# Second attention hands its tiles to the scan inside SBUF; first quarter's norm coefficients alone; softplus by tanh

## The chip, the cores and the metric

One core of one Trainium2 chip runs the whole program. The metric is the device time of one execution in microseconds (us); lower is better. The engines are PE (TensorE, matrix multiply), DVE (VectorE), ACT (ScalarE), POOL (GpSimd) and SP (SyncE, which here only issues DMA transfers and waits). Each runs its own instruction stream; semaphores order them.

## The reference

Two layers work on x of 128 batches x 32 steps x 128 features. What the change touches is the end of the second layer's attention and the preparation of its selective scan:

```python
x = x + _L1_xattn_ref(_layernorm(x), ctx, ctx, Wq, bq, Wk, bk, 32, 0)   # attention over 257 context rows
x = x + _L1_attn_ref(_layernorm(x), W_in, conv_w, conv_b, W_x, W_dt, b_dt, A_log, ...)
...
xc, z = (xz[..., :256], xz[..., 256:])          # xz = x @ W_in.T
u = silu(conv over 4 steps of xc + conv_b)
x_dbl = u @ W_x.T                               # 33 columns: 1 for dt, 16 for B, 16 for C
dt = jnp.clip(jax.nn.softplus(dt_raw @ W_dt.T + b_dt), 0.0001, 10.0)
A = -jnp.exp(jnp.minimum(A_log, 5.0))
y = scan over the 32 steps with 16 states per channel, from u, dt, A, B, C
```

Softplus is log(1 + exp(v)). It equals max(v, 0) + log(1 + exp(-|v|)), and also max(v, 0) - log(0.5 + 0.5 tanh(|v| / 2)).

## The kernel before

The stages run one after another: first attention, mixer, experts (layer 0), second attention (`stage_cross1`), then `stage_scan1`, which calls `scan_inputs`, `scan_states` and `stage_tail`. Between stages all engines meet at a barrier and the semaphores are cleared.

**Two layouts.** Up to the second attention a tile of x is 4 batches x 32 steps on the 128 partitions, and there are 32 tiles: `g.x[128, 32, 128]`, where partition b\*32+s of tile t is step s of batch 4t+b. The scan wants the 128 batches on the partitions and the 32 steps as its 32 tiles. Before, the second attention writes each finished tile to a DRAM tensor (`x_mid`, line 1465, one DMA of 64 KB per tile), and `scan_inputs` reads it back into `g.x` in four DMAs of 512 KB, a quarter of the steps each (line 1659).

**The second attention** is a software pipeline over 32 tiles (`step(t, p)` on each engine). SP's step, in this order: the last context row of tile t (line 1446, 4 rows of 512 B into one partition); in odd steps a context tile for t+2 (line 1395) and its transpose for t+4 (line 1389), half a megabyte each; then the output of tile t-3. Even tiles find their context in SBUF already. The waits are for `o_psum` (attention of tile t-2 done, so that a buffer is free), `scores_psum` and `x_sb` (tile t-3 written). SP runs the step in a hardware loop.

**The preparation of the scan** (`scan_inputs`) starts with the layer norm: DVE takes `bn_stats` of the 32 tiles as they land, then eight small instructions and one Sqrt on ACT give the coefficients of all tiles (`norm_coefficients`). Eight weight loads are issued by ACT (`w_in`, 8 loads); when all are in, DVE folds the convolution taps into the input weights (`w_c`, line 1794) and splits the bias row (lines 833 to 841, the last one `si_cb`). PE waits for all that (`prep`), then runs one tile per step: transpose of the normed tile, convolution and gate as matmuls into `c_ps`, transpose of u, `W_x` product. ACT applies Silu (line 1705), copies the transposed tile (line 1708) and writes |v| of dt into `soft` (Abs, line 1712); DVE copies uT and xd, and computes v = w_dt \* xd + b_dt (line 1785); POOL copies u and z out and prepares gates for the first 12 tiles.

**After the last tile** comes the softplus in four quarters of 8 tiles, in two halves, and the clip:

```python
for half in range(2):
    for q in quarters: activation(soft, soft, ACT.Exp, scale=-1.0)      # L1733
    for q in quarters: activation(soft, soft, ACT.Ln, bias=1.0)         # L1737
...
vec.scalar_tensor_tensor(dt, dt, 0.0, soft, ALU.max, ALU.add)           # L1802
vec.tensor_scalar(dt, dt, 1e-4, 10.0, ALU.max, ALU.min)                 # L1804
```

DVE then negates `a` (line 1806), and the stage ends. `scan_states` follows: ACT first makes 24 products `come` (line 1907), then exponentials `decay` (line 1897) for each step.

Of the kernel before, what the change touches and what calls it, by code (L numbers as in the profile page):

```python
# [1397 lines left out]
def stage_cross1(nc, g):  # L1398
# [7 lines left out]
    with ExitStack() as ctx:  # L1406
# [30 lines left out]
        def _(sp):  # L1437
# [182 lines left out]
def scan_inputs(nc, g, uz, dt, xd, a):  # L1620


    with ExitStack() as ctx:
# [25 lines left out]
        waited, abs_sb, exp_sb, ln_sb, soft_sb, clip_sb = (sem(n) for n in ("waited", "abs_sb", "exp_sb", "ln_sb", "soft_sb", "clip_sb"))  # L1649
        block = ctx.enter_context(nc.Block())  # L1650
# [4 lines left out]
        @block.sync  # L1655
        def _(sp):
            for q in range(XQ):
                t = slice(q * QT, (q + 1) * QT)
                sp.dma_start(g.x[:, t, :], g.x_mid[:, t, :]).then_inc(x_in[q], 16)
            load_tail_rows(g, sp)  # L1660
            sp.wait_ge(g.tail.rows_in, 16 * 3)
            sp.wait_ge(g.tail.loaded, 16 * 4)

        @block.tensor
        def _(pe):
# [29 lines left out]

            pe.wait_ge(prep, TAPS + 2 + 9)
            pipeline(pe, step, 2, 1, TAPS)

        @block.scalar
        def _(act):  # L1700
            def step(t, p):
# [24 lines left out]
            act.wait_ge(abs_sb, T)  # L1726
            act.wait_ge(a_step, 1)
            nc.scalar.activation(a[:, :], a[:, :], ACT.Exp).then_inc(a_step, 1)
            for half in range(2):
                quarters = range(half * LN_Q // 2, (half + 1) * LN_Q // 2)  # L1730
                for q in quarters:
                    s = slice(q * LT, (q + 1) * LT)
                    nc.scalar.activation(soft[:, s, :], soft[:, s, :], ACT.Exp, scale=-1.0).then_inc(exp_sb, 1)  # L1733
                for q in quarters:
                    s = slice(q * LT, (q + 1) * LT)
                    act.wait_ge(exp_sb, q + 1)
                    nc.scalar.activation(soft[:, s, :], soft[:, s, :], ACT.Ln, bias=1.0).then_inc(ln_sb, 1)  # L1737

# [31 lines left out]
        def _(dve):  # L1770
            vec = nc.vector

            def step(t, p):
# [7 lines left out]
                if inside(t - 1):  # L1781
# [3 lines left out]
                    vec.scalar_tensor_tensor(dt[:, t - 1, :], w_dt[:, :], xd[:, t - 1, 0:1], b_dt[:, :],  # L1785
                                             ALU.mult, ALU.add).then_inc(dt_sb, 1)
# [4 lines left out]
            vec.memset(cb[:, :], 0.0).then_inc(prep, 1)  # L1791
            dve.wait_ge(w_in, 16 * W_LOADS)
# [3 lines left out]
            dve.wait_ge(prep, 2)  # L1796
            split_row(vec, dve, prep, TAPS + 2, cb3[:, :], rowmask, (c_hi[:, :], c_rest[:, :], c_f[:, :]), cb[0:3, :])
            pipeline(dve, step, 3, 1, TAPS)
            for q in range(LN_Q):
                s = slice(q * LT, (q + 1) * LT)  # L1800
                dve.wait_ge(ln_sb, q + 1)
                vec.scalar_tensor_tensor(dt[:, s, :], dt[:, s, :], 0.0, soft[:, s, :], ALU.max, ALU.add).then_inc(soft_sb, 1)  # L1802
                dve.wait_ge(soft_sb, q + 1)
# [3 lines left out]
            dve.wait_ge(clip_sb, LN_Q)  # L1807

# [782 lines left out]
def build(nc, dram, out):  # L2591
    with ExitStack() as ctx:
# [11 lines left out]
        with ExitStack() as early:  # L2604
            sb = tensor_makers(nc, early, "early")[0]
            g.w_uv, g.w_eo = sb("w_uv", [P, 2, E1]), sb("w_eo", [P, CB, D])
            g.uvb, g.ob = sb("uvb", [P, 2 * E1], BF16), sb("ob", [P, D])
            g.filt, g.dft, g.idft = sb("filt", [FR, E1]), sb("dft", [P, 3, S]), sb("idft", [FR, S])
            g.w_g, g.w_u, g.w_d = sb("w_g", [P, HC, P]), sb("w_u", [P, HC, P]), sb("w_d", [P, HC, D])
            g.w_r, g.spread0 = sb("w_r", [P, NE]), sb("spread0", [P, RC, P], BF16)  # L2610
            g.w_q, g.w_k, g.cross_cols = sb("w_q", [P, D]), sb("w_k", [P, D]), sb("cross_cols", [P, 2])
# [3 lines left out]
            with ExitStack() as kept:  # L2615
# [92 lines left out]
```

## Time and profile before

| | us |
|---|---|
| median of 3 runs (lowest 1869.15, highest 1873.27) | 1869.2 |
| the profiled execution's own time | 1870.31 |
| its span, first to last instruction | 1868.5 |
| second attention, first DMA issue to its last write of x | 904.9 to 1006.6 |
| from there to the first matmul of the scan's preparation | 1006.6 to 1030.8 |
| preparation, tile by tile, to the last dt | 1030.8 to 1149.0 |
| softplus and clip, to the last instruction of the stage | 1149.0 to 1175.1 |
| scan, from its first instruction | 1175.5 |

The times of the lower rows are positions in the span of the one profiled execution. PE is busy for 1580.0 us of the span (85%), DVE 1353.5 (72%), ACT 1034.3 (55%) and POOL 521.2 (28%), but in the two stretches 1006.6 to 1030.8 and 1149.0 to 1175.1 PE does nothing.

### The profile page before, as it was taken

To read this page: it belongs to the slowest core of one execution; us is meant where nothing else is said; L and a number is where in the kernel's file an instruction comes from. 1 tells how busy PE (TensorE), PEld (TensorE's weight loads), DVE (VectorE), ACT (ScalarE), POOL (GpSimd) and SP (SyncE) were. 2 spreads that over 40 slices of the span, in tenths; PEclk is the share of its full clock that TensorE was granted. 3 is DMA by queue.
4 is the path that set the end of the run, shared out by engine and by line. 5 is a ranking of instruction groups with operands and counts; after the bars stand their busy time and mean duration, and the time that the engine had idled before them with its cause. 6 is when DMAs were issued, how large, how long until landed. Compare 5 with 4: busy or idle time off the path is not lost. (4 is left out here: it accounts for less than half of the span.)

```text
span 1868.5 us, 36875 instructions
## 1 busy us (share of the span) xinstructions
PE 1580.0 (85%) x10997; PEld 1031.1 (55%) x11024; DVE 1353.5 (72%) x3801; ACT 1034.3 (55%) x2779; POOL 521.2 (28%) x559
## 2 busy tenths in 40 slices
PE   5999999999998999799895885477777774999999
PEld 2666666666665455466563674366655563444444
DVE  4777777777777666577686444799999996677765
ACT  2666666666665333344332225899999992322321
POOL 1211111111111100000000721688888880322200
PEclk9999999999999999899897898798988886999999
DMA  5011011011010900000366000000000001000000
GB/s 136 24 34 34 23 34 34 23 34 34 23 34 5 349 8 0 1 1 1 97 212 183 0 0 0 1 1 0 0 0 0 0 0 51 1 7 6 12 6 17
DMA packets 69336, 66.48 MB, mean 36 GB/s; under 512 B 5695, under 2 KB 66834, under 8 KB 69266
## 3 DMA queue, kind: packets, MB, share of 16 engines
q1 hardware_dynamic: 66598, 64.00, 11.5%
q10 hardware_dynamic: 2668, 1.62, 0.3%
q8 instruction: 35, 0.57, 0.1%
q14 instruction: 35, 0.29, 0.0%
HBM read 61.41 MB, written 4.19 MB: 35 GB/s over the span
## 5 line engine op out<-in xcount | busy, mean ns | idle before, releaser
L1995 PE MATMUL ss_y_ps<-ss_h,ss_diag 128*128 128x256 f32 x1024 | 264.4, 422 | 133.8 <-ACT sc_dt L1913 93.2
L1995 PEld LDWEIGHTS ss_y_ps<-ss_h,ss_diag 128*128 128x128 f32 x1024 | 215.6, 214 | 182.4 <-issue 79.1
L595 ACT ACTIVATE x_probs<-x_probs,x_neg_max 128x257 f32<-128x257 f32 x512 | 253.5, 498 | 63.2 <-DVE x_neg_max L696 63.2
L696 DVE CUSTOM_DVE_ANT_0 x_probs<-x_s_ps,x_mask_b 128x257 f32<-128x257 f32 x512 | 187.3, 423 | 133.5 <-PE x_s_ps L403 133.5
L1897 ACT ACTIVATE ss_decay<-sc_dt,sc_a 128x256 f32 (+1 forms) x496 | 207.8, 479 | 1.8 <-DVE ss_h L1960 1.8
L1951 DVE SCALAR_TENSOR_TENSOR ss_decay<-ss_decay,ss_h 128x1024 f32<-128x1024 f32 x124 | 152.3, 1228 | 27.7 <-ACT ss_decay L1897 27.4
L1907 ACT ACTIVATE ss_come<-ss_dtu,sc_xd 128x256 f32<-128x256 f32 x384 | 163.6, 512 | 6.6 <-POOL ss_dtu L1853 6.6
L413 PE MATMUL x_pT_ps<-all_ident,x_probs 128*128 128x128 f32 x1024 | 162.4, 282 | 0.6 <-DVE x_pT L703 0.6
L1867 POOL TENSOR_TENSOR ss_diag<-all_ident,sc_xd 128x512 f32<-128x512 f32 x128 | 158.8, 1240 | 12.8 <-PE ss_y_ps L1995 2.9
L703 DVE COPY x_pT<-x_pT_ps 128x512 f32<-128x512 f32 x256 | 161.3, 668 | 0.5 <-PE x_pT_ps L413 0.5
L1960 DVE CUSTOM_DVE_ANT_0 ss_h<-ss_come,ss_decay 128x1024 f32<-128x1024 f32 x124 | 149.9, 1209 | 0.0
L319 POOL TENSOR_TENSOR x_rsum_b<-x_rsum,x_one_col 128x512 f32<-128x512 f32 x32 | 33.3, 1041 | 408.7 <-DVE x_rsum L713 408.7
L1862 POOL TENSOR_SCALAR ss_come<-ss_come 128x1024 f32<-128x1024 f32 x124 | 131.3, 1059 | 39.9 <-ACT ss_come L1907 34.3
L413 PEld LDWEIGHTS x_pT_ps<-all_ident,x_probs 128*128 128x128 f32 x1024 | 115.1, 144 | 45.3 <-issue 43.1
L2484 DVE TENSOR_TENSOR tl_scaled<-tl_xnT,tl_w_ps 128x512 f32<-128x512 f32 x96 | 65.4, 687 | 53.0 <-PE tl_w_ps L2200 35.9
L2206 PE MATMUL tl_h_ps<-tl_scaled,tl_w 128*128 128x512 f32 x192 | 98.6, 595 | 0.4
L2206 PE MATMUL tl_y_ps<-tl_scaled,tl_w 128*128 128x512 f32 x192 | 97.5, 592 | 0.8 <-DVE tl_scaled L2484 0.4
L595 ACT ACTIVATION_READ_ACCUMULATOR x_probs<-x_probs,x_neg_max 128x1 f32 x512 | 96.3, 188 | 0.0
L403 PE MATMUL x_s_ps<-x_kT,x_qblk 32*128 32x257 f32 x1024 | 92.7, 431 | 0.0
L390 PE MATMUL x_m_ps<-x_w_qkv,x_ctx_t 128*128 128x128 f32 x512 | 75.1, 291 | 18.2 <-issue 17.2
L430 PE MATMUL x_o_ps<-x_pT,x_v 128*32 128x128 f32 x2048 | 82.5, 279 | 0.9 <-DVE x_pT L703 0.9
L374 PE MATMUL x_m_ps<-x_ctx_t,x_w_qkv 128*128 128x512 f32 x128 | 71.4, 640 | 11.8 <-DVE x_o_norm L719 11.8
(373 smaller groups left out, 3072.0 us busy)
## 6 DMA issues: line engine op xcount, KB each, us to landing
x_ctx_t<-ctxT SPq DMA_DIRECT2D x48, 514.0 KB, 3.8
kept_ctx_t<-ctxT SPq DMA_DIRECT2D x16, 514.0 KB, 8.2
kept_ctx_n<-ctx SPq DMA_DIRECT2D x16, 512.0 KB, 8.5
x_ctx_n<-ctx SPq DMA_DIRECT2D x16, 512.0 KB, 4.1
all_x<-x SPq DMA_DIRECT2D x4, 512.0 KB, 7.8
x_mid<-all_x SPq DMA_DIRECT2D x32, 64.0 KB, 4.0
all_x<-x_mid SPq DMA_DIRECT2D x4, 512.0 KB, 7.6
out<-all_x SPq DMA_DIRECT2D x8, 256.0 KB, 2.0
```

The lines of the kernel that those rows point to most:

```text
L413: ins = tr(pT_ps[u % 2][:, n * P:(n + 1) * P], probs[p][:, 2 * u + j, k * P:(k + 1) * P], g.ident[:, :])
L595: ins = nc.scalar.activation(probs[p][:, n, :], probs[p][:, n, :], ACT.Exp, scale=-1.0, bias=neg_max[p][:, n:n + 1], accum_out=sums[p][:, ...
L696: vec.tensor_tensor_reduce(probs[p][:, n, :], s_ps[:, c, 0:S2], mask_b[:, :], -1.0, -MASKED, ALU.add, ALU.min, neg_max[p][:, n:n + 1]).the ...
L703: vec.tensor_copy(pT[u % 4][:, :], pT_ps[u % 2][:, :]).then_inc(pT_sb, 1)
L1862: nc.gpsimd.tensor_scalar(c[:, :, :], c[:, :, :], 10.0, -10.0, ALU.min, ALU.max).then_inc(bound_sb, 1)
L1867: nc.gpsimd.tensor_tensor(diag[q][:, :, :], g.ident[:, :].unsqueeze(1).to_broadcast([P, NH, P]), c.unsqueeze(2).to_broadcast([P, NH, P]), ...
L1897: ins = nc.scalar.activation(decay[r][:, m * DI:(m + 1) * DI], dt[:, t, :], ACT.Exp, scale=a[:, s:s + 1])
L1907: ins = nc.scalar.activation(come[q][k % 2][:, m, :], dtu[k % 2][:, :], ACT.Copy, scale=xd[:, t, s:s + 1])
L1951: vec.scalar_tensor_tensor(d[:, :], d[:, :], TINY, h[q][:, :, :].rearrange("p m d -> p (m d)"), ALU.max, ALU.mult).then_inc(kept_psum, 1)
L1960: vec._custom_dve(bass.dve_ops.TENSOR_ADD_SAT, out=h[q][:, :, :].rearrange("p m d -> p (m d)"), in0=come[q][k % 2][:, :, :].rearrange("p m ...
L1995: ins = nc.tensor.matmul(y_ps[p][:, 0:DI], diag[q][:, m, :], h[q][:, m, :], start=(q == 0 and m == 0), stop=(q == NQ - 1 and m == NH - 1))
L2206: mm([h_ps, y_ps][j // ME][:, :], w[:, j, :], scaled[j % 4][:, :], start=(j == 0), stop=(j == ME - 1 or j == MC - 1)).then_inc(product, 1)
```

## The change

1. The second attention's SP moves tile t-3 within SBUF: four DMAs of 16 KB, one per batch, each from 32 partitions (512 B of each) into the one partition of `g.x_by_step` that belongs to that batch. `x_mid` and its four reloads are gone. SP's loop becomes straight code.
2. `g.x_by_step` is a second array of x's size. Until the second attention it is lent to weights of the layers before; the old `g.x` is freed after the attention.
3. The scan's preparation: `bn_stats` and norm coefficients of tiles 0 to 7 first; the other 24 tiles' `bn_stats` come four at a time inside steps -2 to 3, their coefficients (8 DVE instructions, one Sqrt on ACT) between steps 3 and 4. SP issues two of the eight weight loads (`w_in_T`, `w_x`) in the place of the reloads, ACT the other six.
4. Softplus: the clip moves ahead of it, as bounds on v, one DVE instruction per tile; Tanh(|v|/2) is taken per tile on ACT, one step after Abs; after the last tile ACT takes one Ln per quarter and DVE one instruction per quarter. The Exp of `a` comes after the Ln.

```diff
@@ stage_cross1, SP @@
                 if inside(t - 3):
                     sp.wait_ge(x_sb, t - 2)
-                    dst = g.x_mid[bass.ds((t - 3) * BT, BT)].rearrange("b s d -> (b s) d")
-                    sp.dma_start(dst, g.x[:, t - 3, :]).then_inc(x_out, 16)
-            pipeline(sp, step, 4, 3, 4)
-            sp.wait_ge(x_out, 16 * T)
+                    for b in range(BT):
+                        row = (t - 3) * BT + b
+                        sp.dma_start(g.x_by_step[row:row + 1, :, :], g.x[b * S:(b + 1) * S, t - 3, :]).then_inc(x_out, 16)
+            for t in range(-4, T + 3):
+                step(t, t % 4)
+            sp.wait_ge(x_out, 16 * T * BT)
@@ scan_inputs, SP @@
-            for q in range(XQ):
-                t = slice(q * QT, (q + 1) * QT)
-                sp.dma_start(g.x[:, t, :], g.x_mid[:, t, :]).then_inc(x_in[q], 16)
+            sp.dma_start(w_in_T[:, :], g.dram["L1_attn_W_in_T"]).then_inc(w_in, 16)
+            sp.dma_start(w_x[:, :, :], g.dram["L1_attn_W_x_T"].rearrange("(c p) n -> p c n", p=P)).then_inc(w_in, 16)
             load_tail_rows(g, sp)
@@ scan_inputs, ACT @@
+                if inside(t - 3):
+                    act.wait_ge(abs_sb, t - 2)
+                    nc.scalar.activation(soft[:, t - 3, :], soft[:, t - 3, :], ACT.Tanh, scale=0.5).then_inc(tanh_sb, 1)
-            norm_coefficients(nc, g, act, None, ln_step, lnw)
-            pipeline(act, step, 2, 2, TAPS)
+            first_coefficients(nc, g, act, None, ln_step, lnw, slice(0, QT), 0)
+            for t in range(-2, SECOND):
+                step(t, t % TAPS)
+            first_coefficients(nc, g, act, None, ln_step, lnw, slice(QT, T), 1)
...
-            for half in range(2):
...
+            for q in range(LN_Q):
+                t = slice(q * LT, (q + 1) * LT)
+                act.wait_ge(tanh_sb, (q + 1) * LT)
+                nc.scalar.activation(soft[:, t, :], soft[:, t, :], ACT.Ln, scale=0.5, bias=half[:, :]).then_inc(ln_sb, 1)
             act.wait_ge(a_step, 1)
             nc.scalar.activation(a[:, :], a[:, :], ACT.Exp).then_inc(a_step, 1)
@@ scan_inputs, DVE @@
+                    dve.wait_ge(raw_sb, t)
+                    vec.tensor_scalar(dt[:, t - 1, :], dt[:, t - 1, :], DT_LOW, DT_HIGH, ALU.max, ALU.min).then_inc(dt_sb, 1)
-            arrived_stats(nc, g, dve, x_in, stats)
-            norm_coefficients(nc, g, None, dve, ln_step, lnw)
+            moments(range(QT))
+            first_coefficients(nc, g, None, dve, ln_step, lnw, slice(0, QT), 0)
+            step(-3, -3 % TAPS)
...
+            for t in range(-2, SECOND):
+                step(t, t % TAPS)
+                moments(range(QT + (t + 2) * MORE, min(T, QT + (t + 3) * MORE)))
+            dve.wait_ge(stats, T)
+            first_coefficients(nc, g, None, dve, ln_step, lnw, slice(QT, T), 1)
...
-                vec.scalar_tensor_tensor(dt[:, s, :], dt[:, s, :], 0.0, soft[:, s, :], ALU.max, ALU.add).then_inc(soft_sb, 1)
-                vec.tensor_scalar(dt[:, s, :], dt[:, s, :], 1e-4, 10.0, ALU.max, ALU.min).then_inc(clip_sb, 1)
+                vec.scalar_tensor_tensor(dt[:, s, :], dt[:, s, :], 0.0, soft[:, s, :], ALU.max, ALU.subtract).then_inc(soft_sb, 1)
```

On SP, two steps of the second attention in its steady part. Before, inside the loop (`x_ctx_l`, `x_ctx_n`, `x_ctx_t` are the context loads, `x_mid` the tile's way out):

```order
L1446 ISA [waits x1_o_psum]
L1446 DMA x_ctx_l<-ctx 1x4x128
L1395 ISA [waits x1_o_psum]
L1395 DMA x_ctx_n<-ctx 128x4x256
L1389 ISA [waits x1_scores_psum]
L1389 DMA x_ctx_t<-ctxT 128x4x257
L1465 ISA [waits x1_x_sb]
L1465 DMA x_mid<-all_x 128x128
```

Now, the same odd step and the start of the next:

```order
L1447 DMA x_ctx_l<-ctx 1x4x128 [waits x1_o_psum]
L1396 DMA x_ctx_n<-ctx 128x4x256 [waits x1_o_psum]
L1390 DMA x_ctx_t<-ctxT 128x4x257 [waits x1_scores_psum]
L1467 DMA all_x_by_step<-early_x 1x32x128 [waits x1_x_sb]
L1467 DMA all_x_by_step<-early_x 1x32x128 x3
L1447 DMA x_ctx_l<-ctx 1x4x128 [waits x1_o_psum]
```

One way out per step became four, and the next step's context row stands behind all four.

On ACT, the end of the preparation before (`si_soft` holds |v| and what follows from it, `sc_a` the decay rates), with the first rows of the scan:

```order
L1712 ACTIVATE si_soft<-sc_dt 128x256 x4
L1728 ACT_TABLE_LOAD
L1728 ACTIVATE sc_a<-sc_a 128x16
L1733 ACTIVATE si_soft<-si_soft 128x2048 x2
L1737 ACT_TABLE_LOAD
L1737 ACTIVATE si_soft<-si_soft 128x2048 x2
L1733 ACT_TABLE_LOAD
L1733 ACTIVATE si_soft<-si_soft 128x2048 x2
L1737 ACT_TABLE_LOAD
L1737 ACTIVATE si_soft<-si_soft 128x2048 x2
L1907 ACTIVATE ss_come<-ss_dtu,sc_xd 128x256 x24
L1897 ACT_TABLE_LOAD
```

Now, from the last two tiles on (line 1716 is Abs, 1720 Tanh, 1744 Ln, 1746 the Exp of `a`):

```order
L1716 ACTIVATE si_soft<-sc_dt 128x256
L1720 ACTIVATE si_soft<-si_soft 128x256 x2
L1744 ACT_TABLE_LOAD
L1744 ACTIVATE si_soft<-si_soft,si_half 128x2048 x4
L1746 ACT_TABLE_LOAD
L1746 ACTIVATE sc_a<-sc_a 128x16
L1934 ACTIVATE ss_come<-ss_dtu,sc_xd 128x256 x24
L1924 ACTIVATE ss_decay<-sc_dt,sc_a 128x256 x4
```

Four large Exp and four large Ln with four table loads became four large Ln; the table of the scan's exponentials is now loaded ahead of the stage's end. No table load stands between Silu, Copy, Abs and Tanh inside the steps; the only ones there are those around the second Sqrt:

```order
L1716 ACTIVATE si_soft<-sc_dt 128x256
L1720 ACTIVATE si_soft<-si_soft 128x256
L116 ACT_TABLE_LOAD
L116 ACTIVATE si_lnw<-si_lnw 128x24
L1709 ACT_TABLE_LOAD
L1709 ACTIVATE si_u<-si_c_ps 128x512
```

## Rows read from the trace of the kernel before

**Rows 1.** Windows: busy us (instructions) per engine, granted clock, DMA share, GB/s.

```profile
925.63:1006.99 81.36, 79.88 (x1200) 49.80 (x1198) 64.27 (x276) 29.06 (x105) 0.00 (x0) 1.00 0.68 202
1006.99:1030.78 23.79, 0.00 (x0) 0.00 (x1) 13.39 (x58) 1.51 (x2) 0.20 (x1) 0.52 0.55 162
1149.15:1175.52 26.37, 0.00 (x0) 0.00 (x0) 13.97 (x9) 20.49 (x14) 0.00 (x1) 0.54 0.00 0
```

**Rows 2.** Timeline, attention's end to first matmul: start, us, engine, line, count, [idle before].

```profile
1003.67 3.32 SPq L1465 DMA_DIRECT2D x_mid<-all_x  x4
1006.28 0.35 DVE L1584 SCALAR_TENSOR_TENSOR all_x<-x_o_ps,x_rsum,all_x 128x128 f32<-128x128 f32 x1 [1.21 <-PE x_o_ps L1520]
1009.93 2.08 SPq L1659 DMA_DIRECT2D all_x<-x_mid  x4
1014.04 0.37 ACTq L1722 DMA_DIRECT2D si_rowmask<-c_rowmask  x1
1014.76 1.64 DVE L82 BATCH_NORM_STATS2 all_bn<-all_x 128x6 f32<-128x128 f32 x8 [8.13 <-DMA all_x<-x_mid]
...
1025.35 1.43 DVE L1794 TENSOR_TENSOR si_w_c<-si_w_in_T,si_taps 128x256 f32<-128x256 f32 x4 [0.67 <-DMA si_rowmask<-c_rowmask]
1030.00 0.28 DVE L841 CAST si_cb<-si_c_f 3x256 bf16<-3x256 f32 x1
1030.81 0.44 PE L1672 MATMUL si_x_ps<-all_ident,si_xn 128*128 128x128 f32 x1 [24.60 <-DVE si_xn L1776]
```

**Rows 3.** Timeline from the last dt to the end of the preparation, DVE and ACT.

```profile
1148.55 0.48 DVE L1785 SCALAR_TENSOR_TENSOR sc_dt<-si_w_dt,sc_xd,si_b_dt 128x256 f32<-128x256 f32 x1
1149.15 0.42 ACT L1712 ACTIVATE si_soft<-sc_dt 128x256 f32<-128x256 f32 x1 [0.56 <-DVE sc_dt L1785]
1149.59 1.28 ACT L1728 ACT_TABLE_LOAD   x1
1151.00 3.69 ACT L1733 ACTIVATE si_soft<-si_soft 128x2048 f32<-128x2048 f32 x2
1157.95 2.29 DVE L1802 SCALAR_TENSOR_TENSOR sc_dt<-sc_dt,si_soft 128x2048 f32<-128x2048 f32 x1 [8.91 <-ACT si_soft L1737]
1174.92 0.17 DVE L1806 TENSOR_SCALAR sc_a<-sc_a 128x16 f32<-128x16 f32 x1
```

**Rows 4.** Timeline, start of the scan.

```profile
1186.07 1.28 ACT L1897 ACT_TABLE_LOAD   x1
1189.06 1.23 DVE L1951 SCALAR_TENSOR_TENSOR ss_decay<-ss_decay,ss_h 128x1024 f32<-128x1024 f32 x1 [5.34 <-ACT ss_decay L1897]
```

**Rows 5.** Timeline, one step of the preparation on ACT.

```profile
1134.82 0.60 ACT L1705 ACTIVATE si_u<-si_c_ps 128x512 f32<-128x512 f32 x1 [2.51 <-PE si_c_ps L1681]
```

**Rows 6.** Timeline of SP, one pair of steps of the second attention.

```profile
964.31 0.61 SPq L1446 DMA_DIRECT2D x_ctx_l<-ctx  x1
965.14 0.41 SPq L1395 DMA_DIRECT2D x_ctx_n<-ctx  x1
970.00 0.61 SPq L1446 DMA_DIRECT2D x_ctx_l<-ctx  x1
```

**Rows 7.** DMA issues by line: count, duration ns min/median/max, first and last start us.

```profile
L1465 SPq DMA_DIRECT2D x_mid<-all_x x32: 340/377/1793, 925.6 to 1006.7; - x32
DMA to landing us min/median/max: 1.6/4.0/4.8
L1446 SPq DMA_DIRECT2D x_ctx_l<-ctx x32: 573/614/687, 906.8 to 1003.0; - x32
L288 SPq DMA_DIRECT2D early_uvb<-x_row_p x3: 578/582/591, 552.1 to 553.3; - x3
DMA to landing us min/median/max: 2.5/2.9/3.4
L242 SPq DMA_DIRECT2D early_idft<-c_idft x3: 421/421/585, 18.9 to 20.0; - x3
```

**Rows 8.** Timeline of SP near the program's start.

```profile
18.93 1.51 SPq L242 DMA_DIRECT2D early_idft<-c_idft  x3
```

More of the change, by code:

```diff
@@ L1 @@
+import itertools
 import numpy as np
@@ L1602 @@
 LN_Q = 4
+SECOND, MORE = 4, 4
+DT_LOW, DT_HIGH = float(np.log(np.expm1(1e-4))), float(np.log(np.expm1(10.0)))
 def stage_scan1(nc, g):
@@ L1639, in scan_inputs @@
         soft = sb("soft", [P, T, DI])
+        half = sb("half", [P, 1])
         x_ps, c_ps, u_ps, d_ps = (ps(n, [P, BANK]) for n in ("x_ps", "c_ps", "u_ps", "d_ps"))
         c_ps = [c_ps, ps("c_ps1", [P, BANK])]
-        x_in = [sem(f"x_in{q}") for q in range(XQ)]
         w_in, stats, ln_step, prep = (sem(n) for n in ("w_in", "stats", "ln_step", "prep"))
@@ L1648, in scan_inputs @@
         waited_pool = sem("waited_pool")
-        waited, abs_sb, exp_sb, ln_sb, soft_sb, clip_sb = (sem(n) for n in ("waited", "abs_sb", "exp_sb", "ln_sb", "soft_sb", "clip_sb"))
+        waited, abs_sb, tanh_sb, ln_sb, soft_sb, raw_sb = (sem(n) for n in ("waited", "abs_sb", "tanh_sb", "ln_sb", "soft_sb", "raw_sb"))
         block = ctx.enter_context(nc.Block())
@@ L1694, in step @@
                     ins.then_inc(xd_psum, 1)
-            pe.wait_ge(prep, TAPS + 2 + 9)
+            pe.wait_ge(prep, TAPS + 3 + 9)
             pipeline(pe, step, 2, 1, TAPS)
@@ L1722, in _ @@
             nc.scalar.dma_start(rowmask[:, :], g.dram["c_rowmask"]).then_inc(w_in, 16)
-            norm_coefficients(nc, g, act, None, ln_step, lnw)
-            pipeline(act, step, 2, 2, TAPS)
-            act.wait_ge(abs_sb, T)
+            first_coefficients(nc, g, act, None, ln_step, lnw, slice(0, QT), 0)
+            for t in range(-2, SECOND):
+                step(t, t % TAPS)
+            first_coefficients(nc, g, act, None, ln_step, lnw, slice(QT, T), 1)
+            for t in range(SECOND, 2 * TAPS):
+                step(t, t % TAPS)
+            with act.Fori(0, T // TAPS - 3) as i:
+                for p in range(TAPS):
+                    step(i * TAPS + (2 * TAPS + p), p)
+            for t in range(T - TAPS, T + 3):
+                step(t, t % TAPS)
+            for q in range(LN_Q):
+                t = slice(q * LT, (q + 1) * LT)
+                act.wait_ge(tanh_sb, (q + 1) * LT)
+                nc.scalar.activation(soft[:, t, :], soft[:, t, :], ACT.Ln, scale=0.5, bias=half[:, :]).then_inc(ln_sb, 1)
             act.wait_ge(a_step, 1)
             nc.scalar.activation(a[:, :], a[:, :], ACT.Exp).then_inc(a_step, 1)
-            for half in range(2):
[L1730 to L1737, printed above, removed]
         @block.gpsimd
@@ L1785, in step, with moments @@
                     vec.scalar_tensor_tensor(dt[:, t - 1, :], w_dt[:, :], xd[:, t - 1, 0:1], b_dt[:, :],
-                                             ALU.mult, ALU.add).then_inc(dt_sb, 1)
-            arrived_stats(nc, g, dve, x_in, stats)
-            norm_coefficients(nc, g, None, dve, ln_step, lnw)
+                                             ALU.mult, ALU.add).then_inc(raw_sb, 1)
+                    dve.wait_ge(raw_sb, t)
+                    vec.tensor_scalar(dt[:, t - 1, :], dt[:, t - 1, :], DT_LOW, DT_HIGH, ALU.max, ALU.min).then_inc(dt_sb, 1)
+            def moments(tiles):
+                for k in tiles:
+                    vec.bn_stats(g.bn[:, k, :], g.x[:, k, :]).then_inc(stats, 1)
+            moments(range(QT))
+            dve.wait_ge(stats, QT)
+            first_coefficients(nc, g, None, dve, ln_step, lnw, slice(0, QT), 0)
+            step(-3, -3 % TAPS)
             vec.memset(ones[:, :], 1.0).then_inc(prep, 1)
             vec.memset(cb[:, :], 0.0).then_inc(prep, 1)
+            vec.memset(half[:, :], 0.5).then_inc(prep, 1)
             dve.wait_ge(w_in, 16 * W_LOADS)
@@ L1795, in _ @@
             vec.tensor_scalar(a[:, :], a[:, :], 5.0, None, ALU.min).then_inc(a_step, 1)
-            dve.wait_ge(prep, 2)
-            split_row(vec, dve, prep, TAPS + 2, cb3[:, :], rowmask, (c_hi[:, :], c_rest[:, :], c_f[:, :]), cb[0:3, :])
-            pipeline(dve, step, 3, 1, TAPS)
+            dve.wait_ge(prep, 3)
+            split_row(vec, dve, prep, TAPS + 3, cb3[:, :], rowmask, (c_hi[:, :], c_rest[:, :], c_f[:, :]), cb[0:3, :])
+            for t in range(-2, SECOND):
+                step(t, t % TAPS)
+                moments(range(QT + (t + 2) * MORE, min(T, QT + (t + 3) * MORE)))
+            dve.wait_ge(stats, T)
+            first_coefficients(nc, g, None, dve, ln_step, lnw, slice(QT, T), 1)
+            for t in range(SECOND, 2 * TAPS):
+                step(t, t % TAPS)
+            with dve.Fori(0, T // TAPS - 3) as i:
+                for p in range(TAPS):
+                    step(i * TAPS + (2 * TAPS + p), p)
+            for t in range(T - TAPS, T + 1):
+                step(t, t % TAPS)
             for q in range(LN_Q):
@@ L2596, in build @@
         g.sems = []
-        g.x_mid = nc.dram_tensor("x_mid", (NB, S, D), F32).ap()
         sb = tensor_makers(nc, ctx, "all")[0]
-        g.x = sb("x", [P, T, D])
+        g.x_by_step = sb("x_by_step", [P, T, D])
         g.bn = sb("bn", [P, T, 6])
@@ L2605, in build @@
             sb = tensor_makers(nc, early, "early")[0]
[L2606 to L2610, printed above, removed]
+            g.x = sb("x", [P, T, D])
+            lent = itertools.accumulate([0, 2 * E1, CB * D, D, E1, 3 * S, S, HC * P, HC * P, HC * D, NE])
+            room = g.x_by_step[:, :, :].rearrange("p t d -> p (t d)")
+            first = list(lent)
+            part = [room[:, a:b] for a, b in zip(first, first[1:])]
+            g.w_uv, g.w_eo = part[0].rearrange("p (a n) -> p a n", a=2), part[1].rearrange("p (c n) -> p c n", c=CB)
+            g.ob, g.filt, g.dft, g.idft = part[2], part[3][0:FR], part[4].rearrange("p (a n) -> p a n", a=3), part[5][0:FR]
+            g.w_g, g.w_u, g.w_d = (part[n].rearrange("p (h n) -> p h n", h=HC) for n in (6, 7, 8))
+            g.w_r = part[9]
+            g.uvb, g.spread0 = sb("uvb", [P, 2 * E1], BF16), sb("spread0", [P, RC, P], BF16)
             g.w_q, g.w_k, g.cross_cols = sb("w_q", [P, D]), sb("w_k", [P, D]), sb("cross_cols", [P, 2])
@@ L2623, in build @@
         clear_semaphores(nc, g)
+        g.x = g.x_by_step
         stage_scan1(nc, g)
```

6 lines of the change are left out of this document (2 added, 4 removed).

## Prediction

> **What bounds the kernel now.** I read the windows by stretch first, then the timeline at both gaps, then the DMA issues by line. In the second attention's steady part PE is the bound: it is busy 79.88 of 81.36 us at a granted clock of 1.00 (2.4 GHz), while the DMA engines are busy for a share of 0.68 at 202 GB/s [rows 1]. Two context-row issues on SP 5.69 us apart [rows 6] are one pair of tiles, so 2.85 us per tile. SP has little to do in that time: one context row at 0.614, one write of x at 0.377 and, every second step, two large issues near 0.41 [rows 6, 7]. It waits for the other engines.
>
> Between the last x (1006.28 + 0.35 = 1006.63) and the first transpose (1030.81) PE idles 24.60 us [rows 2]. The last write is issued by 1006.99 and has landed, with the barrier behind it, by 1009.93, when the reload starts. `bn_stats` waits for the reload. The fold of the weights at 1025.35 waits for the last weight, `rowmask`, though it was issued at 1014.04. From there DVE's chain to `cb` ends at 1030.28, and PE starts half a microsecond later [rows 2]. The granted clock in this gap is 0.52 [rows 1], the lower level (1.2 GHz).
>
> The preparation takes 118 us for 32 tiles and a little filling (1030.81 to 1148.55, [rows 2, 3]), some 3.6 us a step, in which ACT is idle 2.51 before its Silu and waits for PE [rows 5]. From the last dt (1149.03) to the last instruction (1175.09) are 26.06 us [rows 3]: DVE waits 8.91 us for Exp and Ln of the first half, then the two engines hand quarters over. ACT is busy for 20.49 us of it and DVE for 13.97 [rows 1], neither full. The scan's first update has DVE idle 5.34 us for ACT, with a table load of 1.28 in it [rows 4].
>
> **The change, part by part.** The profiled execution took 1870.31 us against a median of 1869.2; the 1.1 is carried over, so differences are applied to the median.
>
> *1. Moves on SP.* From the first write at 925.6 [rows 7] SP now issues 128 moves instead of 32. Counted in the code, 28 context rows and 25 half-megabyte loads stand among them. A gap between issues is (1.51 - 0.421 - 0.421 - 0.585) / 2 = 0.04 [rows 7, 8]. So rows cost 28 x 0.65 = 18.2 us and loads 25 x 0.45 = 11.25. A move itself isn't in the trace. The nearest rows by source, 32 rows of a tile, are `idft` at 0.421; `x_mid` with 128 rows shows 0.377; by destination, one partition, they are `uvb` at 0.582 (SBUF to SBUF) and `ctx_l` at 0.614 (only 4 rows) [rows 7]. I take 0.42, since the instruction's pattern is 32 rows of 512 B on one side as for `idft`: 128 x 0.46 = 58.9, sum 88.3, end 925.6 + 88.3 = 1013.9 instead of 1006.99: **+6.9**. So SP replaces PE as the bound of this stretch, by little. The bounds: nothing can end before the last x and its four moves, 1006.63 + 4 x 0.42 = 1008.3, +1.4, reached at 0.377 a move; at 0.582 it is +27.7 and at 0.614 +31.8. Every 0.01 us in a move's issue is 1.3 us. What queues behind the moves is the next context row; PE waits for it when SP falls behind.
>
> *2. Landing.* The last move must land before the barrier: `uvb` takes 2.5 us at least where `x_mid` takes 1.6 at least [rows 7]. Taken as **+0.5**, between 0 and 1.3.
>
> *3. Front of the preparation.* Without the reload the weights share the queues with nothing. In the gap 162 GB/s x 23.79 us = 3.85 MB moved, of which the reload is 32 x 64 KB = 2.1 MB, 54%. DMA busy time was 0.55 x 23.79 = 13.1 us [rows 1], so 7.1 us of it goes. The fold then starts 15.42 - 7.1 = 8.3 us after the stage's start. The first tiles' statistics (1.64 us for eight, [rows 2]) and coefficients are over by then, and the first normed tile is ready ahead of the fold, so behind `cb` only a semaphore's 0.1 is left: 8.3 + 4.93 + 0.1 = 13.3 instead of 20.88. ACT issues two loads less, taken as 0.15 more: **-7.7**. Bounds: the last issue at +4.1, 0.9 earlier for the two loads given away, and 0.37 + 1.6 to land, +5.2, give -10.6; one microsecond of bytes less saved gives -6.6.
>
> *4. Second Sqrt in the pipeline.* The rest of the statistics, 4 x 0.205 a step (1.64 / 8, [rows 2]), lies in DVE's idle time of six steps. The Sqrt costs ACT two table loads of 1.28 and one small activation, at most 0.42 (Abs, [rows 3]): 3.0 us, plus the wait for DVE's six small instructions ahead of it, near 1. Behind it on ACT stand the Silu and the copy of the next tile, which PE waits for. ACT has 2.51 spare per step [rows 5], so **+1.5**, between 0 (buffers carry it) and 2.9 (a DVE chain that comes late).
>
> *5. Tanh and clip inside the steps: 0.* Tanh is 0.42 (taken from Abs) inside ACT's 2.51 idle; the clip, half of a dt instruction to all of it (0.2 to 0.48, [rows 3]), is hidden behind PE. If PE were not the bound, both would cost 32 x 0.42 = 13 us each at most; only the 32nd is on the path, and is counted next.
>
> *6. After the last dt.* Clip with its hops 0.9, Abs 0.42, Tanh 0.42, table load 1.28, a first Ln of 1.9 (two large Exp take 3.69; 1151.00 to 1157.95 is these, a load, a hop, and 1.85 for Ln), then DVE's four at 2.29, which is longer than ACT's 1.9, so DVE paces: 9.16; `a` 0.17, three hops 0.4 [rows 3]. Sum 14.65 instead of 26.06: **-11.4**, between -9.5 (an ordering wait per quarter) and -12.
>
> *7. Scan start.* The exponential's table is loaded beside DVE's last quarters, so the 1.28 at 1186.07 goes [rows 4]: **-1.3**, or 0 if DVE's wait is not on it.
>
> Sum: 6.9 + 0.5 - 7.7 + 1.5 - 11.4 - 1.3 = **-11.5, so 1857.7 us**. With each term at its own bound, and moves of 0.377 to 0.42, it lies between -22 and -5; since not all fall on one side, 1848 to 1864 is the range of this case.
>
> **Rivals.**
>
> *A. The one-partition destination sets the issue price.* For: both rows with one destination partition are the dearest, 0.58 and 0.61, though `ctx_l` has only four rows. Against: `idft`'s third issue took 0.585 as well, so the figure may be a queue's state. Then term 1 is +27.7 to +31.8 in place of +6.9, and the sum +9.3 to +13.4: 1878 to 1883, slower. The change breaks even where the moves cost 11.5 / 128 = 0.09 more than 0.42, at 0.51 us an issue. Chance 0.22.
>
> *B. The DMA engines become the bound.* A tile moves 202 x 2.85 = 576 KB, of which `x_mid` is 64, 11%. Without it the share would be 0.68 x 0.89 = 0.605, and 0.395 x 2.85 = 1.13 us per tile are free on each engine. The four moves are 128 pieces of 512 B, 8 per engine, so it decides at 141 ns a piece. `x_mid`'s own share comes to 0.11 x 0.68 x 2.85 / 8 = 27 ns a piece, which speaks against this; that all pieces of a move end in one partition, where no row shows the rate, speaks for it. At twice the deciding price a tile takes 2.85 + 1.13 = 3.98 us and 28 tiles 32 us more, in place of term 1: 1869.2 - 11.5 - 6.9 + 32 = 1883. Chance 0.12.
> The Trainium skill's page SBUF — State Buffer, section "Door 1: The DMA port swizzle", says that DMA bandwidth depends on how many of the 16 ports the partitions reach, and its formula puts four neighbouring partitions, a tile's batches, at one port. From its 435 GB/s for all ports, an estimate by that page is 27 GB/s for one: 2.4 us for a tile's moves and 1.2 us for the port's share of the 512 KB of context, 3.6 in place of 2.85, which over 28 tiles and in place of term 1 would give 1872; where the next tile's other port takes over meanwhile, it would give nothing. No row of this trace shows a transfer into one port at length.
>
> *C. The weights come no earlier, or the issue price lies at 0.45 to 0.54.* For the first: the last issue was at 1014.04 and the wait ended 11 us later; if what lasted was not the reload's bytes but the other loads, which copy one row to 128 partitions, term 3 is 0 and the sum -3.8: 1865. For the second, +3.8 to +15.4 on the sum: 1862 to 1873. Against the first is the share of bytes above. Both end near no change. Chance 0.13; in it the change does not do what it says in one of its parts.
>
> The case summed above has 0.50. The other 0.03 are more than one term at its favourable bound, below 1848.
>
> **How the numbers follow.** 0.3%, 5.6 us, is about what a measurement of this kernel can tell from no change: 1863.6 to 1874.8. The case of 0.50 lies almost whole below it, and its 0.03 that does not is made up by the 0.03 below 1848: faster 0.50. C is most of the same, 0.13. A and B are 0.34, and the 0.03 left over, a dear move with smaller gains elsewhere, makes slower 0.37. The range must reach from 1848 to 1884, since A and B hold a third.
>
> **What the changed profile would show.** Term 1: the issue duration of line 1467, near 0.42, and the spacing of the context rows still near 5.7 to 5.9 us per pair; with A it reads 0.58 or more and PE's idle time ends on `ctx_l`; with B the issue is short, the DMA share nears 1 and the landing grows far over 3.4 us. Term 3: the first transpose 13 us after the stage's first instruction, with the fold at 8. Term 4: six table loads between the stage's start and the scan instead of seven in the same stretch, and one longer step about tile 4. Term 6: 14.7 us from the last dt to `a`, with DVE's four instructions back to back. Term 7: no table load at the first `decay`. The prediction is wrong if the moves' issue is not within 0.38 to 0.45, if the fold still waits 15 us, or if a step of the preparation grows by the Tanh and the clip, which would show as PE idle on ACT or DVE in every step.

## The result, and the profile after

The changed kernel takes 1897.0 us (median of 4 runs, 1896.0 to 1898.9) against 1870.0 before: a ratio of 1.014, 95% interval 1.0126 to 1.0155, 27 us slower. The prediction said 1857.7, with a range of 1848 to 1884; the time lies outside it, above rivals A and B. The medians below leave out one of half_all's five runs, which took 1930.5 us at a granted clock of 0.857 where the others had 0.944 to 0.947.

Three windows of the changed kernel's trace answer to [rows 1]: the moves, the gap to the first transpose, and the end of the preparation (columns as there: busy us of PE, PEld, DVE, ACT and POOL, granted clock, DMA share, GB/s).

```profile
923.93:1045.25 121.32, 96.34 (x1200) 57.76 (x1198) 64.81 (x276) 29.05 (x105) 0.00 (x0) 0.80 0.51 136
1045.25:1064.85 19.60, 0.00 (x0) 0.00 (x0) 8.07 (x35) 1.49 (x2) 0.20 (x1) 0.50 0.42 87
...
1188.89:1202.71 13.82, 0.00 (x0) 0.00 (x0) 9.29 (x7) 11.69 (x11) 0.00 (x0) 0.56 0.00 1
```

The first row holds more than the whole loss: from the first move to the last, 121.32 us where the same stretch took 81.36. The same 1200 matmuls are in it. The DMA engines are less busy than before, 0.51 against 0.68, and so is PE, 96 of 121 us, at a granted clock of 0.80 in place of 1.00. What was busy shows in the timeline of SP, two steps of it, and in the line of the moves' issues (count, ns min/median/max):

```profile
1010.30 0.62 SPq L1447 DMA_DIRECT2D x_ctx_l<-ctx  x1
1010.97 0.44 SPq L1396 DMA_DIRECT2D x_ctx_n<-ctx  x1
1011.45 0.51 SPq L1390 DMA_DIRECT2D x_ctx_t<-ctxT  x1
1012.00 2.42 SPq L1467 DMA_DIRECT2D all_x_by_step<-early_x  x4
1014.46 0.62 SPq L1447 DMA_DIRECT2D x_ctx_l<-ctx  x1
1015.12 3.89 SPq L1467 DMA_DIRECT2D all_x_by_step<-early_x  x4
1019.06 0.63 SPq L1447 DMA_DIRECT2D x_ctx_l<-ctx  x1
```

```profile
L1467 SPq DMA_DIRECT2D all_x_by_step<-early_x x128: 514/591/2070, 923.9 to 1044.7; - x128
```

SP has almost no gap left: each start above is the end before it plus 0.04, and over the whole stretch only two of 180 gaps are longer than 0.05, 0.37 and 0.77 us. In [rows 6] it had one context row every 2.85 us and waited in between. SP's own waits in the stretch (in total us, times, longest) say the same; they were 19.5 us before and are 5.4 now:

```profile
SPq L1447 <- PE x_o_ps L1523: 2.1, 4, 0.8
SPq L1390 <- PE x_s_ps L1500: 1.2, 1, 1.2
SPq L1396 <- PE x_o_ps L1523: 1.2, 3, 0.5
SPq L1467 <- DVE early_x L1587: 0.9, 2, 0.5
```

The other parts, in the timeline of the front, of the second Sqrt on ACT, and of the end (answering to [rows 2] and [rows 3]):

```profile
1059.87 1.43 DVE L1812 TENSOR_TENSOR si_w_c<-si_w_in_T,si_taps 128x256 f32<-128x256 f32 x4 [6.01 <-DMA si_rowmask<-c_rowmask]
...
1064.85 0.47 PE L1676 MATMUL si_x_ps<-all_ident,si_xn 128*128 128x128 f32 x1 [26.01 <-DVE si_cb L842]
```

```profile
1083.26 0.60 ACT L1709 ACTIVATE si_u<-si_c_ps 128x512 f32<-128x512 f32 x1 [2.51 <-PE si_c_ps L1685]
...
1084.65 1.28 ACT L116 ACT_TABLE_LOAD   x1
1088.55 0.22 ACT L116 ACTIVATE si_lnw<-si_lnw 128x24 f32<-128x24 f32 x1 [2.61 <-DVE si_lnw L126]
1088.79 1.28 ACT L1709 ACT_TABLE_LOAD   x1
1090.08 0.60 ACT L1709 ACTIVATE si_u<-si_c_ps 128x512 f32<-128x512 f32 x1
...
1095.35 0.60 ACT L1709 ACTIVATE si_u<-si_c_ps 128x512 f32<-128x512 f32 x1 [3.89 <-PE si_c_ps L1685]
```

```profile
1193.72 8.90 DVE L1831 SCALAR_TENSOR_TENSOR sc_dt<-sc_dt,si_soft 128x2048 f32<-128x2048 f32 x4 [4.49 <-ACT si_soft L1744]
1202.54 0.17 DVE L1833 TENSOR_SCALAR sc_a<-sc_a 128x16 f32<-128x16 f32 x1
...
1215.26 1.23 DVE L1978 SCALAR_TENSOR_TENSOR ss_decay<-ss_decay,ss_h 128x1024 f32<-128x1024 f32 x1 [3.92 <-ACT ss_decay L1924]
```

In the first, the fold still waits for `rowmask`, but only 11.3 us after the stage's start at 1048.54. In the second, the Silu after the Sqrt starts 6.8 us behind the one before it, where a step is 3.6, and the next one 5.3 behind that. In the third, DVE's four instructions stand back to back, 13.8 us after the last dt all of it is done, and no table load is left ahead of the scan's first update.

Between the same marks in both traces the span's growth of 26.2 us (1868.5 to 1894.7) comes apart like this:

| part | before | after | difference | predicted |
|---|---|---|---|---|
| up to the first move | 925.63 | 923.93 | -1.7 | 0 |
| first to last move issued (1) | 81.4 | 121.3 | +40.0 | +6.9 |
| landing and barrier (2) | 2.9 | 3.3 | +0.3 | +0.5 |
| stage start to first transpose (3) | 20.9 | 16.3 | -4.6 | -7.7 |
| first transpose to last dt (4, 5) | 118.2 | 124.0 | +5.8 | +1.5 |
| last dt to `a` (6) | 26.1 | 13.8 | -12.2 | -11.4 |
| `a` to the scan's first update (7) | 14.0 | 12.6 | -1.4 | -1.3 |

The first line isn't the change's: in the traces of all kernels below the second attention begins anywhere between 902.6 and 907.2.

### The profile page after: what moved, and what is told of

The parts are those of the page before. It is cut to its first block and busy times, and to the rows that moved or that the text cites. A ratio compares the mean times of both kernels' runs of the same rounds, so it can differ in the third digit from the quotient of the medians.

```text
span 1894.7 us, 36853 instructions
## 1 busy us (share of the span) xinstructions
PE 1596.5 (84%) x10997; PEld 1040.1 (55%) x11024; DVE 1363.0 (72%) x3838; ACT 1035.8 (55%) x2807; POOL 523.9 (28%) x559
## 3 DMA queue, kind: packets, MB, share of 16 engines
q1 hardware_dynamic: 67974, 62.20, 11.4%
## 5 line engine op out<-in xcount | busy, mean ns | idle before, releaser
L596 ACT ACTIVATION_READ_ACCUMULATOR x_probs<-x_probs,x_neg_max 128x1 f32 x512 | 96.3, 188 | 0.0
```

Of the source, the lines that this page charges most:

```text
L596: ins = nc.scalar.activation(probs[p][:, n, :], probs[p][:, n, :], ACT.Exp, scale=-1.0, bias=neg_max[p][:, n:n + 1], accum_out=sums[p][:, ...
```

## The experiments

Each ran on one chip beside the kernel before, whose median was between 1868.5 and 1869.8 in these runs. The column "moves" is the time from the first issue of a tile's way out to the end of the last one, whichever engine issues it, "prep" from the first transpose to the last dt, both from the one profiled execution (in half_on_act it took 1880.5 us, 8 above the median); the ratio is to the kernel before, with its interval.

| kernel | us | ratio | moves | prep |
|---|---|---|---|---|
| before | 1870.0 | | 81.4 | 118.2 |
| changed | 1897.0 | 1.014 (1.0126 to 1.0155) | 121.3 | 124.0 |
| one_move | 1888.2 | 1.009 (1.006 to 1.012) | 108.9 | 124.1 |
| half_on_act | 1872.4 | 1.001 (1.000 to 1.003) | 101.2 | 124.1 |
| after_early | 1897.6 | 1.015 (1.014 to 1.017) | 119.6 | 124.7 |
| half_early | 1862.1 | 0.996 (0.995 to 0.998) | 87.3 | 124.1 |
| one_early | 1862.1 | 0.996 (0.995 to 0.998) | 84.8 | 124.5 |
| all_coefs | 1892.7 | 1.012 (1.010 to 1.013) | 124.5 | 119.1 |
| softplus_only | 1855.3 | 0.992 (0.990 to 0.994) | 81.4 | 118.6 |
| half_all | 1853.7 | 0.992 (0.990 to 0.995) | 87.5 | 118.9 |
| soft_pre | 1854.5 | 0.991 (0.989 to 0.994) | 88.5 | 118.6 |
| soft_pre_early | 1851.7 | 0.990 (0.989 to 0.992) | 82.9 | 119.3 |

**Who sets the pace of the moves?** Theory 1: SP's issuing. Theory 2: the transfers, as in rival B. Two edits, each leaving the bytes and the destination alone. In the first, one DMA per tile:

```diff
-                    for b in range(BT):
-                        row = (t - 3) * BT + b
-                        sp.dma_start(g.x_by_step[row:row + 1, :, :], g.x[b * S:(b + 1) * S, t - 3, :]).then_inc(x_out, 16)
+                    row = (t - 3) * BT
+                    sp.dma_start(g.x_by_step[row:row + BT, :, :], g.x[:, t - 3, :]).then_inc(x_out, 16)
```

> The changed kernel with one DMA per tile in place of four: 128 rows of 512 B into four partitions, the same bytes and pieces, a quarter of the issues. Theory 1, SP's issuing sets the pace (128 issues of 0.63 us on average fill the 121 us of the stretch): a pair of steps then takes SP about 2 x 0.6 + 2 x 0.66 + 0.44 + 0.67 = 3.6 us of the 5.69 that PE needs, PE binds again, the stretch falls from 121.4 to about 82 us, and the time from 1897.0 to about 1858. Theory 2, the transfers into few partitions set the pace and hold the issues up: the bytes and the destination are the same, so the stretch stays near 121 us and the time above 1890.

In the second, batches 0 and 1 of a tile stay with SP, ACT's loop becomes straight code too, and ACT's step gets, behind its exponential (the edit in part):

```diff
+                if inside(t - 3):
+                    act.wait_ge(x_sb, t - 2)
+                    for b in range(BT // 2, BT):
+                        row = (t - 3) * BT + b
+                        nc.scalar.dma_start(g.x_by_step[row:row + 1, :, :], g.x[b * S:(b + 1) * S, t - 3, :]).then_inc(x_out, 16)
```

> The changed kernel with the same 128 moves, two of each tile's four issued by ACT (behind its exponential of the step) instead of SP. Theory 1, SP's issuing: SP needs 4 x 0.63 + 2 x 0.66 + 1.1 = 4.95 us of 5.69 per pair, ACT 1.27 of its idle time per tile, so PE binds again, the stretch falls to about 83 us and the time to about 1859. Theory 2, the transfers themselves: their number, size and destination are unchanged, so the time stays above 1890. A third outcome, near 1875: ACT's issues delay its exponentials, which PE waits for.

Both fell between the two theories: 1888.2 and 1872.4, the second near its third outcome. SP was no longer full (it waited 59.1 us in one_move's stretch and 25.9 in half_on_act's, where the changed kernel has 5.4), yet PE waited. The timeline of one_move shows where (SP and PE, in order of time):

```profile
925.34 0.61 SPq L1447 DMA_DIRECT2D x_ctx_l<-ctx  x1
...
925.99 0.60 SPq L1466 DMA_DIRECT2D all_x_by_step<-early_x  x1
...
928.20 0.58 SPq L1447 DMA_DIRECT2D x_ctx_l<-ctx  x1
...
932.06 0.65 PE L1522 MATMUL x_o_ps<-kept_ctx_n,x_pT 128*32 128x128 f32 x16 [1.97 <-issue]
```

This product takes its context from tiles kept in SBUF, so the one transfer it can wait for is its context row, issued at 925.34, 6.7 us earlier. The window of the same trace in which almost only moved pieces ran:

```profile
928.25:929.70 1.45, 1.45 (x17) 1.02 (x17) 0.95 (x5) 0.54 (x2) 0.00 (x0) 1.00 0.31 34
```

34 GB/s with 0.31 of the DMA engines busy: the pieces of these moves ran at a sixth of the 202 GB/s of [rows 1]. So a third theory: with SP relieved, PE waits for the context row, which stands in the DMA queue behind other transfers. The test gives that row two more tiles of time (four buffers), in all three kernels (the edit in part):

```diff
-                if inside(t):
+                if inside(t) and inside(t + 2):
                     wait(sp, o_psum, t - 1)
-                    load_l(t, p)
+                    load_l(t + 2, p + 2)
```

> The changed kernel, all four moves on SP, with the context row two tiles earlier. Theory: here SP's issuing is the bound, it issues the same number, so the stretch stays at 120 us or so and the time at 1893 to 1898. Rival: the late context row was the bound here too, and SP was only seen busy since it was never ahead: 1860 to 1875.

> Two of the four moves on ACT as in the run of that edit, and the last context row loaded two tiles earlier into four buffers instead of two. Theory: with half of the moves on ACT, SP kept pace, and what was left (PE waited before its output product with nothing running on its suppliers, up to 2.2 us at a time, and its granted clock fell) was the context row, queued in the DMA rings behind loads and moves; two tiles earlier it is always there: the stretch comes to 82 to 84 us and the time to about 1860. Rival: PE waited for something else (the loads of half a megabyte, or ACT held up by its own issues): no change, 1866 to 1880.

> One DMA of 128 rows per tile, and the context row two tiles earlier. Theory: the one DMA's 128 pieces ran on a few engines at about 17 pieces per 0.25 us and took up to 4 us for two tiles, the context row waited behind them, and PE for it; two tiles earlier it has that time: 1858 to 1865, against 1888 without. Rival: the slow pieces also hold up the loads of the context, or are themselves the bound: 1875 to 1888.

All three came out by the theory: 1897.6 where SP issues all moves, 1862.1 and 1862.1 where it doesn't. This also settles half_on_act's third outcome: half_early has the same issues on ACT, so it was not these that cost the 10 us between the two. In half_early the stretch to the next stage's start has PE at its full rate again almost throughout:

```profile
923.90:1013.96 90.06, 81.66 (x1216) 51.03 (x1215) 65.74 (x280) 29.63 (x107) 0.00 (x1) 0.97 0.67 184
```

So the changed kernel is bound by SP's issuing, and behind that bound stood a second one, the late context row. That the row is late by its place in the queue is read from the one_move rows; the test shows only that it was late.

**What makes an issue dear?** One run, with five forms of move side by side in the place of the four:

> One look at prices: in place of a tile's four moves stand moves of five forms, 32 rows of 512 B into one partition (as in the change), 32 rows into 32 partitions, 8 rows into one partition (four of them), 32 rows to DRAM, and, for the first 16 tiles, 64 rows into two partitions. The tiles are therefore put in wrong places and the attention stretch is longer; only the issue durations by line are read. Theory, one destination partition is what makes an issue dear: 32 to one 0.59, 8 to one near 0.59, 64 to two near 0.59, 32 to 32 near 0.42, to DRAM 0.38 to 0.42. Rival 1, every short move from SBUF to SBUF is dear: 32 to 32 also 0.59 and only DRAM cheap. Rival 2, the price grows with the rows that go into one partition: 8 to one near 0.45, 32 to one 0.59.

The issue durations by line, in the order 32 rows to one partition, 32 to 32, 8 to one, 32 to DRAM, 64 to two:

```profile
L1466 SPq DMA_DIRECT2D all_x_by_step<-early_x x32: 531/540/567, 927.8 to 1108.9; - x32
L1467 SPq DMA_DIRECT2D all_x_by_step<-early_x x32: 584/591/592, 928.4 to 1109.5; - x32
L1469 SPq DMA_DIRECT2D all_x_by_step<-early_x x128: 625/639/1287, 929.0 to 1112.2; - x128
L1471 SPq DMA_DIRECT2D x_mid<-early_x x32: 430/437/834, 931.8 to 1112.8; - x32
L1473 SPq DMA_DIRECT2D all_x_by_step<-early_x x16: 585/585/609, 932.3 to 1027.1; - x16
```

The theory of the single destination partition fell: 32 rows into 32 partitions cost as much, 0.591, and 8 rows into one more, 0.639. Rival 1 fits: a short move from SBUF to SBUF costs 0.54 to 0.64 whatever its partitions, the same rows to DRAM 0.437. Why is open, and two other things move a price by as much as 0.1. One is the place in the row: in the changed kernel the first of a tile's four moves took 0.515 as a rule, the other three 0.591, and the five forms were tried in one order only. The other is the loop: the same `x_mid` writes took 0.376 in soft_pre, where SP runs a loop, and 0.446 in soft_pre_early, where it runs straight code, and the same `x_ctx_t` loads 0.403 and 0.506; in return the gap between issues went from 0.27 to 0.045. The prices of `x_mid` and of the context loads in [rows 7] are such loop prices.

**The preparation.** Statistics and coefficients of all tiles ahead, one Sqrt, on the changed kernel:

```diff
-            moments(range(QT))
-            dve.wait_ge(stats, QT)
-            first_coefficients(nc, g, None, dve, ln_step, lnw, slice(0, QT), 0)
+            moments(range(T))
+            dve.wait_ge(stats, T)
+            first_coefficients(nc, g, None, dve, ln_step, lnw, slice(0, T), 0)
```

> The changed kernel with the statistics and coefficients of all 32 tiles ahead of the first step, one Sqrt, as before the change; the moves as changed. Theory: the second Sqrt with its two table loads and DVE's coefficients inside the steps is what lengthened the preparation from 118.2 to 124.0 us, and 24 more statistics (4.9 us) fit into the 6.0 us in which DVE waits for the weights: about 5 us less, 1892. Rival: the Tanh and the clip in each step lengthened it, and the front waits for the statistics: no gain, 1896 or above.

1892.7, 4.3 us less; the preparation takes 119.1 in place of 124.0. So the second Sqrt, with the statistics and coefficients that go with it, cost 4.9 us. Of the remaining 0.9, Tanh and clip make 0.3: in softplus_only, the next run, the steps are as long as before and only the last dt comes 0.3 later. Most of the other 0.6 lies in the third step, which takes 3.8 us in all_coefs and 3.15 before; the reason is open.

**The softplus alone** on the kernel before (the fourth part of the change, its diff as shown ahead of the prediction, all else untouched):

> The kernel before with the changed softplus alone (clip ahead, Tanh per tile, one Ln per quarter), tiles through DRAM and one norm as before. Theory: the end of the preparation gives 12.2 us and the scan's first table load 1.4, the clip behind the last tile takes 0.9 back: 1870 - 12.7 = 1857. Rival: in the changed kernel the steps hid Tanh and clip only because other things were late, and each step grows by 0.1 to 0.4 us: 1860 to 1870.

1855.3: by itself this part gives 14.4 us. In the trace its own places give 13.3 of it (12.2 and 1.4 behind the last dt, 0.3 lost ahead of it).

**Towards a better kernel.** On half_early, all coefficients at once, and the tail's rows issued behind the preparation's weights:

```diff
+            sp.wait_ge(w_in, 16 * W_LOADS)
             load_tail_rows(g, sp)
```

> Two moves per tile on ACT with the context row two tiles earlier (1862.1), and in the preparation the coefficients of all tiles at once as in that run, and the three rows and three weights of the tail issued by SP only when the preparation's own weights are in. Theory: the single Sqrt gives 4.5 to 5 us as it did alone, and the weights, which shared their queues with the tail's copies of one row to 128 partitions, arrive 2 to 3 us sooner: 1862.1 - 4.9 - 2.5 = 1855. Rival: the weights are late by their own pieces, and the later tail rows hold up POOL's gates and then the first steps: 1857 to 1862.

1853.7, where the theory had 1855; the first transpose comes 13.8 us after the stage's start. Moves within SBUF, with all that they need, thus end level with softplus_only, which leaves them out.

On softplus_only, the weights in the last four steps of the attention:

```diff
+                if isinstance(t, int) and T - 4 <= t < T:
+                    for k in (2 * (t - T + 4), 2 * (t - T + 4) + 1):
+                        nc.scalar.dma_start(*loads[k]).then_inc(scan_in, 16)
```

> The kernel before with the changed softplus alone (1855.3), and the eight weights of the preparation loaded by ACT in the last four steps of the second attention, into room that weights of earlier layers no longer need (the scan's and the tail's working tiles lie there later); DVE folds them before the statistics. Tiles still go through DRAM. Theory: the weights are what the first transpose waited for; without them it waits for the reload's last quarter (9.2 us after the stage's start), 3.2 us of statistics behind it, 1.9 of coefficients and one normed tile: 14.7 us instead of 20.9: 1855.3 - 6.2 = 1849. Rival: the loads in the last four steps delay the context that the attention waits for, or the end of the stage, and take half of it back: 1852 to 1855.

1854.5, the rival's: the attention lost the 7 us that the front won. Half of it is one wait on PE for a context row, the rest stands behind it, where the granted clock was 0.60 (997.0 to 1017.0) and 16 products took 1.08 us instead of 0.65:

```profile
1003.52 1.08 PE L1521 MATMUL x_o_ps<-kept_ctx_n,x_pT 128*32 128x128 f32 x16 [3.66 <-issue]
```

> The last kernel (changed softplus, weights loaded in the last four steps of the second attention, 1854.5), with the context row loaded two tiles earlier into four buffers. Theory: there PE waited 3.66 us once, at 1003.5, for a context row queued behind the broadcast weights, and the attention ended some 4 us late; with the row two tiles earlier the front's 6 us stay won: 1850. Rival: the half-megabyte context loads are behind the broadcast weights just as well, or SP, now straight code, loses the 4 us again at the stage's end: 1853 to 1856.

1851.7, 0.990 of the kernel before (0.9886 to 0.9919), faster than both kernels of the case. The first transpose comes 14.0 us after the stage's start. 1850 was expected; one wait of 2.2 us for `ctx_n`, near the same place, is left. The 2.9 us against soft_pre are little next to soft_pre's own spread (1851.5 to 1857.1).

## Why the prediction was wrong

**Term 1 failed, in its choice of a row.** The mechanism was named (SP's issuing replaces PE as the bound; every 0.01 us is 1.3 us), and after_early against half_early shows it. The step that failed is "I take 0.42, since the instruction's pattern is 32 rows of 512 B on one side as for `idft`". The moves cost 0.591 at the median, outside the 0.38 to 0.45 that the prediction named as its own test. The one row of [rows 7] with the same two ends, SBUF to SBUF, was `uvb` at 0.582; it was put with rival A for its one destination partition, which price_forms shows to be the wrong reason for the right number. Of the 128 issues 119 took 0.51 to 0.61, 0.573 on average; at this price, with 0.04 between them, the 128 moves take 78.5 us instead of 58.9, +19.6.

**And the sum lacked a term.** Of the other 13 us of the 33 by which term 1 was short, 9.9 are eleven issues, nine moves and two `x_ctx_t`, that took 0.84 to 2.07 us; one of them is in the 3.89 at 1015.12 above. (The last 3.5 are SP's two waits, and context loads and rows that took somewhat longer than taken.) The DMA queues of the stretch (packets, MB, share) hold ten loads of 16 KB of instructions:

```profile
q1 hardware_dynamic: 20528, 16.31, 49.7%
q8 instruction: 10, 0.16, 0.7%
```

In the trace each of the ten begins within 0.6 us of the start of a long issue (at one of them two neighbouring issues are long). Before, the stretch has ten such loads as well, but only three met an issue over 0.9 us (the longest is the 1.793 of `x_mid` in [rows 7]), and SP had time. That the loads hold up the issue was not tested, and they are not all of it: in one_early 25 issues took over 0.8 us, and 16 of these stand beside no load. What makes an issue long stays open.

**Rival A** (0.22) had the price right, though not its reason, and gave 1878 to 1883; the long issues, and terms 3 and 4, put the result 14 us above it. **Rival B** (0.12) did not occur: the DMA share fell to 0.51, half_early makes the same 128 transfers in 87.3 us, and a move's 32 pieces (16 KB) went through in a quarter of a microsecond, as this window of the changed kernel shows (66 GB/s):

```profile
962.25:962.50 0.25, 0.25 (x6) 0.25 (x4) 0.25 (x2) 0.09 (x1) 0.00 (x0) 1.00 0.28 66
```

The estimate of 27 GB/s for one port, worked out from the Trainium skill's page SBUF — State Buffer, section "Door 1: The DMA port swizzle", does not agree with this row; the row is one short move, and a long transfer into one port was not tried.

**Term 3** was -4.6, not -7.7. Its direction was right: without the reload the fold starts earlier, 11.3 us after the stage's start in place of 15.4. But "7.1 us of it goes", the reload's share of the bytes, was too much; the weights still share their queue with the tail's rows, which all_coefs and half_all show: with the tail's rows ahead of them DVE has the last weight 11.5 us after the stage's start, with the rows behind them at 8.8 it no longer waits.

**Term 4** was mis-sized: +4.9 instead of +1.5, above its own bound of 2.9. ACT waits 2.61 us for DVE's coefficients with the Sqrt's table already loaded; the Silu behind it comes at 1090.08 where 1086.84 was due (1083.26 and a step of 3.58), and the next is later again by 1.7. The premise "a DVE chain that comes late" was taken for the bad end and is what happened. **Term 5** was almost right: 0.3 us behind the last tiles, nothing in the steps (softplus_only).

**Terms 2, 6 and 7** held: +0.3, -12.2 and -1.4. DVE paces the four quarters, 8.90 us back to back, as the prediction had it, and softplus_only has the same 13.8 us from the last dt to `a`.

Without terms 1 and 4 the sum was right in sign and near in size: terms 2, 3, 6 and 7 were put at -19.9 and came to -17.9. softplus_only, which has terms 5 to 7 alone, took 1855.3.

## What to carry to other kernels

Price an issue by a row with the same two memories, not the same shape, and from straight code if the new issues will stand in straight code; and when a count is multiplied by four and every 0.01 us is 1.3 us, give the whole span between candidate rows to the main case. An engine that issues transfers is an engine with a load: add its issues per step against the step, with room for the long ones. When a queue gets more traffic, look at the smallest load in it that something waits for, and give it a buffer or two more: here that alone was worth 10 and 26 us, once the first bound was gone, and nothing before.

## What the runs showed of the hardware

- The issue of a short SBUF to SBUF move usually took 0.51 to 0.64 us with 1, 2, 4 or 32 destination partitions; the same rows to DRAM 0.437.
- The same DMA took longer to issue in straight code than in a loop on SP: `x_mid` 0.446 against 0.376, `x_ctx_t` 0.506 against 0.403.
- In the changed kernel's attention an issue took 0.84 to 2.07 us at each of the ten moments when 16 KB of instructions were loaded; in one_early 16 issues over 0.8 us came without such a load.
- DMAs of 128 rows into four partitions ran at 34 GB/s with 0.31 of the DMA engines busy; one of 32 rows into one partition at 66 GB/s, with 0.28. What decides how many engines take part was not tried.
- The granted clock fell with PE's waits: 1.00 before, 0.80 in the changed kernel's attention, where the same 1200 matmuls took 96.3 us instead of 79.9, and 0.97 again in half_early.
